# The row of softmax maxima placed by one DMA from VectorE's results, and the attention outputs in two PSUM banks

## The reference, cut to what matters

```
x = x + xattn(layernorm(x), ctx)
  q = latents @ Wq.T          # per head [512, 96]
  k = concat(ctx, latents) @ Wk.T   # 576 positions
  v = concat(ctx, latents) @ Wv.T
  attn = softmax(q @ k.T / sqrt(96))
  out  = (attn @ v) @ Wo.T
x = x + ffn(layernorm(x))
```

## Time and profile before

| | |
|---|---|
| median of three runs | 2153.96 us |
| the profiled execution | 2154.07 us, span 2152.3 us |
| TensorE matmuls busy (PE) | 2127.9 us, 99% |
| TensorE weight loads (PEld) | 1750.1 us, 81% |
| VectorE (DVE) | 803.2 us, 37% |
| ScalarE (ACT) | 696.3 us, 32% |
| GpSimd (POOL) | 692.3 us, 32% |

### The profile page before, as it was taken

One profiled execution on the slowest core, in us unless ns is written; L12 is line 12 of the kernel. 1 busy time (PEld: TensorE's weight loads), 2 busy tenths in 40 slices (PEclk: granted clock), 3 DMA queues, 4 the chain that ended last, 5 costly groups with the idle time before them and its releaser, 6 DMA issues.

```text
span 2152.3 us, 30567 instructions
## 1 busy us (share of the span) xinstructions
PE 2127.9 (99%) x9820; PEld 1750.1 (81%) x9820; DVE 803.2 (37%) x1410; ACT 696.3 (32%) x1206; POOL 692.3 (32%) x568
## 2 busy tenths in 40 slices
PE   8999999999999999999999999999999999999998
PEld 7888888877777777778888878787878888888886
DVE  4322222178787778750100313222221232222222
ACT  5111111157777777761111222211123311111111
POOL 2500000136777767663122433010014422222221
PEclk9999999999999999999999999999999999999999
DMA  5642322625555555534433435222124532222222
GB/s 193 215 148 88 127 88 89 183 79 146 147 135 156 140 146 134 142 93 145 147 115 130 165 115 175 98 81 94 63 73 132 187 115 83 84 86 83 84 87 72
DMA packets 230940, 261.62 MB, mean 122 GB/s; under 512 B 76496, under 2 KB 144336, under 8 KB 230736
## 3 DMA queue, kind: packets, MB, share of 16 engines
q1 hardware_dynamic: 186016, 188.70, 28.6%
q10 hardware_dynamic: 44848, 71.97, 10.9%
HBM read 168.07 MB, written 92.27 MB: 121 GB/s over the span
## 4 chain that ended last, share of the span: by engine, by line
PE 97%; DVE 1%; issue 1%; ACT 1%; DMA 0%; POOL 0%; SPq 0%; DVEq 0%; ACTq 0%; POOLq 0%
PE psum L116 30%; PE psum L117 29%; PE psum L118 29%; PE psum L896 4%; PE psum L227 1%; PE psum L947 1%; PE psum L931 1%; PE psum L930 1%; PE psum L948 1%; PE psum L1561 0%; PE psum L1560 0%; PE psum L903 0%; DMA staging<-in_x 0%; DVE small L179 0%; ACT operands L236 0%
## 5 line engine op out<-in xcount | busy, mean ns | idle before, releaser
L116 PE MATMUL psum<-operands 128*128 128x512 f32 (+3 forms) x2888 | 1124.1, 389 | 11.4 <-DVE operands L342 9.4
L117 PE MATMUL psum<-operands 128*128 128x512 f32 (+3 forms) x2888 | 1110.6, 385 | 0.0
L118 PE MATMUL psum<-operands 128*128 128x512 f32 (+3 forms) x2888 | 1109.1, 384 | 0.0
L116 PEld LDWEIGHTS psum<-operands 128*128 128x128 f32 (+1 forms) x2888 | 543.9, 188 | 118.4 <-DVE operands L342 8.8
L118 PEld LDWEIGHTS psum<-operands 128*128 128x128 f32 (+1 forms) x2888 | 544.3, 188 | 106.8
L117 PEld LDWEIGHTS psum<-operands 128*128 128x128 f32 (+1 forms) x2888 | 545.2, 189 | 93.4
L1189 POOL TENSOR_TENSOR operands<-staging,operands 128x512 fp32r<-128x512 f32 x92 | 118.2, 1295 | 368.0 <-ACT operands L1184 367.8
L1075 DVE TENSOR_REDUCE small<-psum 128x1 f32<-128x576 f32 x256 | 192.1, 750 | 99.9 <-PE psum L896 99.8
L1788 POOL TENSOR_TENSOR operands<-operands 128x640 fp32r<-128x640 f32 x64 | 100.4, 1574 | 318.7 <-ACT operands L1783 318.3
L817 POOL TENSOR_TENSOR operands<-staging,operands 128x512 fp32r<-128x512 f32 x128 | 164.0, 1288 | 35.7 <-ACT operands L997 26.9
L1640 DVE TENSOR_TENSOR staging<-staging 128x512 f32<-128x512 f32 x64 | 45.5, 729 | 304.6 <-ACT staging L1606 303.8
(11 more groups left out here) (107 smaller groups left out, 1357.6 us busy)
## 6 DMA issues: line engine op xcount, KB each, us to landing
h_scratch<-staging ACTq DMA_DIRECT2D x80, 256.0 KB, 2.2
operands<-h_scratch SPq DMA_DIRECT2D x64, 320.0 KB, 3.1
operands<-recip_scratch SPq DMA_DIRECT2D x64, 192.0 KB, 4.2
o_scratch<-staging SPq DMA_DIRECT2D x64, 192.0 KB, 4.8
operands<-o_scratch SPq DMA_DIRECT2D x64, 192.0 KB, 2.7
operands<-q_hi_scratch ACTq DMA_DIRECT2D x14, 768.0 KB, 6.0
operands<-q_lo_scratch ACTq DMA_DIRECT2D x14, 768.0 KB, 6.0
staging<-in_x SPq DMA_DIRECT2D x20, 512.0 KB, 3.8
```

Source lines behind the costliest of these rows:

```text
L116: e.matmul(o, lh, rh, start=first, stop=False)
L117: e.matmul(o, lh, rl, start=False, stop=False)
L118: return e.matmul(o, ll, rh, start=False, stop=last)
```

## The change

Four edits, all in stage b:
- A tile u of maxima holds every fourth query (u, u+4, u+8, ...) instead of 128 neighbours. L896 takes its 128 columns of q with a step of four elements, 16 bytes.
- VectorE's maxima of a head then stand as 128 x 4 in the order of the queries, and one DMA lays them from the 128 partitions, 4 values (16 bytes) from each, into row 96. They lie at the end of the operands' memory, with the matmuls' type. The transpose on TensorE, the copy on VectorE and their semaphores are gone. The DMA waits for the fourth maximum, and VectorE's first maximum of a head for the DMA of the head two back, which read the same four columns.
- The bank that the transpose used (2, in part, beside the maxima) is free, and the outputs of even heads go there, those of odd heads stay in bank 6. The first `pv` of a head waits for the copy of the head two back.
- At the edges: the fourth score tile of the first head waits for the maxima of the first three, and the second tile of stage c, which writes bank 2, for the last copy of outputs.

```diff
-        rowst = [mmf(VB + 4 * NT * VW + r * P, P, ST) for r in range(2)]
-        nm = [sm[:, 80 + ST * r:80 + ST * (r + 1)] for r in range(2)]
+        nm = [mmf(22 * SLOT + 1024 + ST * r, ST) for r in range(2)]
...
-        b_oe, b_rcp, b_om = sem("b_o_left", 1), sem("b_recip"), sem("b_o_scaled", 2)
+        b_oe, b_rcp, b_om = sem("b_o_left", 2), sem("b_recip"), sem("b_o_scaled", 2)
...
+        def o_bank(o):
+            return PS[:, 6 if o % 2 else 2, :]
...
             def row_in(i, o):
-                e.wait_ge(*past(b_rw, head(i, o) + 1))
+                e.wait_ge(*past(b_mx, head(i, o) * ST + ST))
                 e.sem_inc(idle, 1)
-                e.dma_start(raw(qp[p][0][HD:HD + 1, a * S:(a + 1) * S]).rearrange("o (u s) -> o u s", u=ST),
-                            raw(rowst[r])).then_inc(b_row[r], 16)
+                e.dma_start(raw(qp[p][0][HD:HD + 1, a * S:(a + 1) * S]).rearrange("o (p u) -> o p u", u=ST),
+                            raw(nm[r])).then_inc(b_row[r], 16)
...
-                m = e.matmul(bank[:, h * TH:(h + 1) * TH], qp[p][0][0:HD, a * S + u * P:a * S + (u + 1) * P],
+                m = e.matmul(bank[:, h * TH:(h + 1) * TH], qp[p][0][0:HD, a * S:(a + 1) * S].rearrange("d (p u) -> d p u", u=ST)[:, :, u],
                              kp[p][0][0:HD, h * TH:(h + 1) * TH], start=True, stop=True)
...
-        def b_pe_row(e, i, o):
-            e.wait_ge(*past(b_mx, head(i, o) * ST + ST))
-            e.wait_ge(*past(b_rw, head(i, o)))
-            e.transpose(PS[0:ST, 2, 0:P], nm[o % 2], ident[:]).then_inc(b_rt, 1)
...
             def pv(i, o, j):
                 if j == 0:
-                    e.wait_ge(*past(b_oe, head(i, o)))
+                    e.wait_ge(*past(b_oe, head(i, o) - 1))
...
-                    parts3(e, PS[:, 6, :], v0, v1, pt[j][0], pt[j][1], j == 0, False).then_inc(b_pt, 1)
+                    parts3(e, o_bank(o), v0, v1, pt[j][0], pt[j][1], j == 0, False).then_inc(b_pt, 1)
...
-            b_pe_row(e, 0, 2)
             for j in range(NT):
+                if j == 3:
+                    e.wait_ge(*past(b_mx, 3 * ST))
                 st(0, 0, j)
...
-                e.activation(ou[o], PS[:, 6, :], ACT.Copy).then_inc(b_oe, 1)
+                e.activation(ou[o], o_bank(o), ACT.Copy).then_inc(b_oe, 1)
...
         def b_dve_max(e, i, o, u, bank=su):
             if u == 0:
-                e.wait_ge(*past(b_rt, head(i, o) - 1))
+                e.wait_ge(*past(b_row[o % 2], 16 * nth(i, o, 2)))
...
-        def b_dve_row(e, i, o):
-            e.wait_ge(*past(b_rt, head(i, o) + 1))
-            e.wait_ge(*past(b_row[o % 2], 16 * nth(i, o, 2)))
-            e.tensor_copy(rowst[o % 2], PS[0:ST, 2, 0:P]).then_inc(b_rw, 1)
...
-                    if to_max:
-                        b_dve_row(e, i, hh + 3)
...
             def tile(b, t, transposes=False):
                 e.wait_ge(*past(cc_x1, b * ST + t - 1))
+                if b * ST + t == 1:
+                    e.wait_ge(*past(b_oe, NH))
```

More of the change, by code:

```diff
@@ L61, in xattn_ffn_kernel @@
         SLOT = 2 * D
-        MM = es.enter_context(nc.sbuf_tensor("operands", [P, 22 * SLOT + 1024], f32r))
+        MM = es.enter_context(nc.sbuf_tensor("operands", [P, 22 * SLOT + 1032], f32r))
         SF = es.enter_context(nc.sbuf_tensor("staging", [P, 6656], f32))
         ident = es.enter_context(nc.sbuf_tensor("ident", [P, P], f32))
-        sm = es.enter_context(nc.sbuf_tensor("small", [P, 344], f32))
+        sm = es.enter_context(nc.sbuf_tensor("small", [P, 336], f32))
         PS = es.enter_context(nc.psum_tensor("psum", [P, 8, NB], f32))
@@ L127, in xattn_ffn_kernel @@
         rt_ps, nt_ps = PS[:, 7, 0:ST], PS[:, 7, 8:8 + ST]
-        nmean = sm[:, 340:344]
+        nmean = sm[:, 80:84]
         def norm_z(tag, xn, last_free, first=(6, 7), tiles=False):
@@ L421, in p0_act @@
             e.wait_ge(*past(ph_start, 2))
-            e.activation(sm[:, 336:337], ident[:, 0:1], ACT.Sqrt)
+            e.activation(sm[:, 84:85], ident[:, 0:1], ACT.Sqrt)
             for n in range(5, 13):
@@ L590, in body @@
                         e.wait_ge(*past(ph_start, 2))
-                        e.activation(sm[:, 336:337], ident[:, 0:1], ACT.Exp)
+                        e.activation(sm[:, 84:85], ident[:, 0:1], ACT.Exp)
                 if not last:
@@ L908, in b_pe_first @@
                 b_pe_max(e, 0, t - 1, k // 2, su_first)
-            if t > 1 and k == ST:
-                b_pe_row(e, 0, t - 2)
         def b_pe(e):
@@ L944, in pv @@
                 if j < ST:
-                    parts3(e, PS[:, 6, :], v0, v1, pt[j][0], pt[j][1], j == 0, False).then_inc(b_pt, 1)
+                    parts3(e, o_bank(o), v0, v1, pt[j][0], pt[j][1], j == 0, False).then_inc(b_pt, 1)
                 else:
-                    e.matmul(PS[:, 6, :], v0, pt[j][0], start=False, stop=False)
-                    e.matmul(PS[:, 6, :], v1, pt[j][0], start=False, stop=True).then_inc(b_pt, 1)
+                    e.matmul(o_bank(o), v0, pt[j][0], start=False, stop=False)
+                    e.matmul(o_bank(o), v1, pt[j][0], start=False, stop=True).then_inc(b_pt, 1)
             def body(i, last):
@@ L954, in body @@
                             st(i, hh + 1, j)
[L955 to L959, removed]
+                        if j < ST and not (last and hh + 3 >= 2 * G):
+                            b_pe_max(e, i, hh + 3, j)
                         if last and hh == 2 * G - 1 and j == 0:
@@ L1072, in b_dve_max @@
             if u == 0:
-                e.wait_ge(*past(b_rt, head(i, o) - 1))
+                e.wait_ge(*past(b_row[o % 2], 16 * nth(i, o, 2)))
             e.wait_ge(*past(b_S, head(i, o) * ST + u + 1))
             e.tensor_reduce(nm[o % 2][:, u:u + 1], bank[:, 0:T], AX.X, ALU.max, negate=True).then_inc(b_mx, 1)
-        def b_dve_row(e, i, o):
-            e.wait_ge(*past(b_rt, head(i, o) + 1))
-            e.wait_ge(*past(b_row[o % 2], 16 * nth(i, o, 2)))
-            e.tensor_copy(rowst[o % 2], PS[0:ST, 2, 0:P]).then_inc(b_rw, 1)
         def b_dve_first(e, t):
             for u in range(ST if t else 0):
-                if t > 1 and u == 2:
-                    b_dve_row(e, 0, t - 2)
                 b_dve_max(e, 0, t - 1, u, su_first)
@@ L1133, in b_dve @@
             split(0, 0, 3)
-            b_dve_row(e, 0, 2)
             add(0, 0)
@@ L1499, in xattn_ffn_kernel @@
         d_gl, d_gt = sem("d_gate_staged"), sem("d_gate_transposed")
-        gTs = sm[:, 216:216 + P]
+        gTs = sm[:, 208:208 + P]
         gT = [gTs[32 * t:32 * t + 2 * NE, :] for t in range(ST)]
```

2 lines of the change are left out of this document (removed).

## The result

The changed kernel takes 2163.74 us (median of 5 runs, 2163.21 to 2165.66) beside 2154.25 us for the kernel before (5 runs, 2153.83 to 2154.8): ratio 1.0046, 95% interval 1.0033 to 1.0059. It is slower by 9.5 us, where I forecast 17 us less; the time lies at the high end of rival 1 (2163), just above my range. The profiled execution has a span of 2161.4 us, 9.1 more than before, at a mean clock of 0.997 (before: 0.998).

A forecast was written before the change was run, and what follows sets the result against it. TensorE was taken to bound the kernel. From 2153.96 us, -8.3 (transposes) -7.6 (second bank) -1.3 (unplaced) +0.5 (last row) -0.3 (start) = -17.0 gave 2137.0 us; range for 8 in 10: 2132 to 2163.

The forecast's parts named there:

- the high end: L896's strided load priced by its 2048-byte span: 0.23 us, second load of each pair sticks out 0.10 us, +26 us.
- rival 1: L896's strided load at half rate, 214 ns for its columns: +23 us, 2160 us in all (2155 to 2163); chance 0.31.
- The strided weights: L896's weight loads with 16 bytes between columns, called the unknown: taken as costing nothing, at most +26 us.
- the low end: L896's strided weight load costs nothing more than the contiguous 189 ns; the price the forecast took.
- Rival 3: TensorE's loads and streams hinder each other, the pair's first load sticks out too: 2188 us; chance 0.08 with other dearer cases.
- The spare: Time L896's loads can grow behind the matmul ahead: 0.12 us for a pair's first, 0.02 us for its second.
- The transposes and the second bank: On TensorE, 64 transposes gone, -8.3 us; first tile's wait for the output copy gone in 63 heads, -7.6 us.
- The unplaced 0.1 us: Part of each head's 0.45 us on TensorE beyond its matmuls, not located; about a fifth credited to the change, -1.3 us.
- The wait at the fourth tile: TensorE's fourth pair waits 0.11 us a head for VectorE's third maximum; claimed to stay.
- VectorE's copy and the first maximum: Dropping VectorE's row copy (17.2 us, counted as nothing) starts the addition 0.2 us earlier, so no new first-tile wait.
- The row's DMA: SyncE's transfer of maxima into the row: 2.6 us to landing, free in the loop, +0.5 us at the end.
- The stage's start: TensorE's idle 0.27 us for the first maximum at the attention stage's start goes with VectorE's copy: -0.3 us.

The follow-up runs named there:

- s2: The changed kernel with a head's four tiles loading 128 queries in steps of 5, 6, 8 and 16 elements: 2164.86 us in one run.
- e5: The changed kernel with tiles of every second query in each half of 256 (8-byte step), the row laid by two DMAs: 2137.13 us.
- e10: e5 with all outputs in one bank (6), waiting for the copy of the head just before: 2152.51 us.
- e9: e5 with VectorE's third maximum between the two parts of its first split, and the loads of values behind the next row's DMAs: 2130.10 us.
- e11: e1 with SyncE's loads of values moved behind the four DMAs of the next row: 2148.93 us.
- e1: The changed kernel with tiles of 128 neighbouring queries again, the row laid by four DMAs of 4-byte pieces: 2155.65 us.

## Why the prediction was wrong, point by point

**The strided weights: this step failed.** "I take the low end. The nearest row is the load of as many columns by the same instruction" put the price at nothing; measured is the high end, 0.10 us for each pair, 25.5 us. Both reasons were weak. That as many columns are loaded says nothing of how they lie, and a stream of neighbours read at 0.45 ns a column shows room for neighbours only. Its high end (+26 us, total +9) was right to 0.5 us, but by luck, for `s2` refutes its reason; rival 1 with 214 ns for the columns was near the measured 230, and its reason, by the lines, is the one that the steps bear out. Rival 3 isn't seen: the first load of a pair stays hidden, for the pair still starts 0.23 us after the matmul ahead (713.51 to 713.74). The spare was worked out rightly: the second load of a pair had 0.02 us, and so nearly all that it grew was paid.

**The transposes and the second bank: right together, wrong apart.** -8.3 and -7.6 us stand against -9.0 and -8.6 in the changed kernel's starts; `e5`, with both and without the stride, landed on the sum. But they overlap in time: the first without the second is worth nothing that can be told (`e10`). I had read two waits 1.5 us apart as independent. The sum came out all the same, because the change takes both.

**The unplaced 0.1 us: there was none.** I gave 1.3 us of it to the change, and up to 6 us of it to the low end of the range. A head of `e9`, in which none of the three waits is left, takes 7.58 us, and 7.58 + 0.13 + 0.13 + 0.11 is the 7.95 of before. My 7.5 was low by rounding: in `e9` the start distance is 0.233 us on average and not 0.23, and a pair takes 0.266. The 1.3 us were right in size only because the two waits were each a little longer than I had read them (+1.7 us together).

**The wait at the fourth tile: right, it stays.** The profile's idle column would have misled here: what L896's load waits for VectorE fell from 17.9 to 6.9 us, since a slower load leaves less time idle, while the starts still show the 0.11 us and `e9` gets it back. Go by starts, not by the idle column.

**VectorE's copy and the first maximum: right.** The addition at 713.68 and the maximum at 714.31 follow each other without a gap and TensorE's first tile shows no wait; the 17 us of VectorE show no gain of their own (no run takes the copy away alone). A slip beside it: by the earlier trace rows VectorE has 1.6 us of a head free, not 1.4.

```profile
713.68 0.68 DVE L1087 TENSOR_TENSOR psum<-psum,staging 64x512 f32<-64x512 f32 x1
714.31 0.76 DVE L1066 TENSOR_REDUCE operands<-psum 128x1 fp32r<-128x576 f32 x1
```

**The row's DMA: wrong in size, right in effect.** I took 2.6 us to landing; it is 3.9, inside the bounds (2.6 to 4.5):

```profile
operands<-operands SPq DMA_DIRECT2D x64, 2.0 KB, 3.9
```

In the loop nobody waits for it. At the last head TensorE does:

```profile
953.59 0.40 PE L941 MATMUL psum<-operands 128*128 128x512 f32 x1
955.30 0.50 PE L115 MATMUL psum<-operands 97*128 97x512 f32 x1 [1.31 <-DMA operands<-operands]
```

1.71 us between these starts against 1.47 before (944.67 to 946.14): +0.24 us, forecast +0.5.

**The stage's start: about half of it.** I expected 0.3 us back. The second pair still starts late:

```profile
456.12 0.39 PE L117 MATMUL psum<-operands 97*128 97x512 f32 x1
456.49 0.76 PE L896 MATMUL psum<-operands 96*128 96x288 f32 x2
457.08 0.40 PE L115 MATMUL psum<-operands 128*128 128x512 f32 x1
```

From the matmul ahead of the pair to the one behind it is 0.96 us, 0.37 more than the undisturbed 0.23 + 0.36. Before the change it was 1.03 (455.12 to 456.15), 0.54 more than the 0.23 + 0.26 of then. So 0.17 us came back.

## What to carry to other kernels

Price an access pattern that no row shows by what it touches, not by how many elements it moves: here 128 columns in steps of 16 bytes cost 123 ns more a load than neighbours, and steps of 8 bytes cost 7. A weight load is free only as long as the matmul ahead of it lasts; where that is short (288 columns, 0.13 us) nearly all that the load grows is paid. Where a wait's end is counted from an earlier event, work that lies between the two is free, and taking it out wins nothing until the wait goes too (`e10`). And a DMA that a loop's first instruction waits for goes ahead of the bulk loads in its queue, in few issues: with four, the bulk loads came late in their turn (`e11`).

## What the runs showed of the hardware

- The weight load of 128 columns of 4 bytes on 96 partitions: 189, 196, 254, 320, 306, 304, 322 and 308 ns in steps of 1, 2, 3, 4, 5, 6, 8 and 16 elements.
- A wait of 3.07 us on TensorE was followed by some 7 us at a mean granted clock of 0.51 (from 548 to 555 us in `e1`), so that it cost twice its length; four of 2.5 to 2.6 us in that run were followed by about half of that. The length of the wait alone doesn't tell: 2.98 us at the last head of `e1` was not followed by a lower clock, 3.35 us there in `e11` was (0.52 from 933 to 940 us), and 2.10 us in `e5` too (0.57 from 930 to 934 us). Waits of 0.8 to 1.9 us in the attention stage were followed by none (`e1`, `e11`, `e9`, `e10`, the changed kernel).
- A DMA of 128 pieces takes SyncE 0.5 to 0.6 us to issue, whether the pieces have 16, 8 or 4 bytes (0.53 us at 707.37 in the changed kernel, 1.20 us for two in `e5`, 2.47 us for four in `e1`). What a row costs the queue goes by the number of DMAs here.
